# Attention over eight rows: 128x128 scores replaced by 32x32 diagonal blocks, with a block transpose on VectorE

## What is computed

```python
x -> layer_norm -> (S=8, B=512, D=256); H = 4 heads of 64
qkv = x @ Wqkv.T + bqkv
scores = einsum('bhqd,bhkd->bhqk', q, k) * (1/sqrt(64))   # 8 x 8 for each position and head
att = softmax(scores);  o = einsum('bhqk,bhkd->bhqd', att, v)
y = layer_norm(x + o @ Wo.T + bo);  idx = argmax(y @ Wg.T)   # the row's expert
```

## Time and profile before

| | us |
|---|---|
| median of 3 runs (lowest, highest) | 1231.37 (1230.73, 1235.14) |
| span of the profiled execution | 1231.3 |
| PE busy in the span | 1156.3 (94%) |
| DVE, ACT, POOL busy | 762.9 (62%), 529.5 (43%), 506.5 (41%) |
| mixing, 688.4 to 929 us | 240.6 |

### The profile page before, as it was taken

The page is one execution under the profiler, slowest core; times in us unless marked ns, Lnnn a source line. Parts: engine busy times, 40 slices in busy tenths (PEclk is TensorE's granted clock), DMA queues, the critical chain, the costliest instruction groups (busy, mean ns, idle before and its releaser), DMA issues. The chain is left out here.

```text
span 1231.3 us, 27541 instructions
## 1 busy us (share of the span) xinstructions
PE 1156.3 (94%) x8847; PEld 785.6 (64%) x8848; DVE 762.9 (62%) x2136; ACT 529.5 (43%) x1123; POOL 506.5 (41%) x718
## 2 busy tenths in 40 slices
PE   8999999999999999999898999999999999999995
PEld 3546455464554645546454466666667999999995
DVE  4555667757767577665635557666674565556653
ACT  5445454545454544545452255544433333333330
POOL 3334325244152442433421122444353556655664
PEclk9999999999999999999999999999999999999998
DMA  7284654644737346374273123434313111111110
GB/s 217 74 222 123 176 148 121 177 117 133 186 99 200 85 136 183 89 194 112 78 199 85 50 78 103 142 134 162 110 41 98 51 42 51 50 55 51 52 44 7
DMA packets 142637, 137.83 MB, mean 112 GB/s; under 512 B 29545, under 2 KB 135919, under 8 KB 142449
## 3 DMA queue, kind: packets, MB, share of 16 engines
q1 hardware_dynamic: 136976, 124.23, 36.2%
q0 software_dynamic: 5280, 12.66, 3.0%
q10 hardware_dynamic: 320, 0.16, 0.1%
HBM read 49.41 MB, written 50.83 MB: 81 GB/s over the span
## 5 line engine op out<-in xcount | busy, mean ns | idle before, releaser
L972 ACT ACTIVATE probs<-ps_b 128x512 f32<-128x512 f32 (+2 forms) x352 | 174.5, 538 | 91.8 <-PE ps_b L1439 36.5
L593 POOL TENSOR_SCALAR_AFFINE_SELECT probs<-probs 128x512 f32<-128x512 f32 x128 | 82.1, 641 | 267.8 <-ACT probs L972 264.5
L2840 PE MATMUL ps_c<-keep_w,e_hT 128*128 x624 | 141.0, 379 | 0.0
L2840 PEld LDWEIGHTS ps_c<-keep_w,e_hT 128*128 128x128 f32 x624 | 115.7, 190 | 14.1
L714 DVE CUSTOM_DVE_ANT_0 ps_a<-ps_a,mask_qk 128x256 f32<-128x256 f32 x224 | 88.9, 450 | 18.8 <-PE ps_a L1263 18.7
L708 DVE TENSOR_REDUCE top<-ps_a 128x2 f32<-128x512 f32 (+1 forms) x112 | 74.1, 683 | 30.1 <-PE ps_a L1263 29.3
L1263 PE MATMUL ps_a<-k_rows,q_rows 96*128 96x256 bf16 (+1 forms) x512 | 84.9, 262 | 4.6 <-DVE top L714 2.7
L1819 ACT ACTIVATE e_w_now<-keep_w 128x1024 f32 x78 | 78.1, 1049 | 22.0 <-issue 12.1
L2800 ACT ACTIVATE e_yT<-ps_d 128x256 f32<-128x256 f32 x39 | 14.9, 383 | 167.8 <-PE ps_d L2819 167.8
L2829 PE MATMUL ps_a<-e_yT,e_w_now 128*128 128x128 f32 x640 | 76.1, 278 | 0.0
L1294 PE MATMUL ps_b<-q_rows,k_rows 98*128 98x256 bf16 (+1 forms) x512 | 75.7, 261 | 0.2
(11 more groups left out here) (248 smaller groups left out, 2470.4 us busy)
## 6 DMA issues: line engine op xcount, KB each, us to landing
...
```

The lines of the kernel that those rows point to most:

```text
L593: nc.gpsimd.affine_select(own, own, [[0, TILES], [1, P]], ALU.is_ge, keep_zero, base=0, channel_multiplier=-1).then_inc(probs_cut.sem, 1)
L972: nc.scalar.activation(probs[:, user % 2, lo:lo + width], ps_exp[:, f % 2, 0:width], ACT.Exp).then_inc(exp_done.sem, 1)
L2840: mm = nc.tensor.matmul(ps_out[:, s, 0:D], hT[:, s, f, :], w2[:, bass.ds(e * KF * D + f * D, D)], start=(f == 0), stop=(f == KF - 1))
```

## The change

The rows of a tile are laid out by position (`x_in[s:P:B]`: row p is sequence row p % 8 of position p // 8), so the 8 rows of a position are neighbours and a 32x32 block on the diagonal holds four whole positions. Scores are computed for the four diagonal blocks of each tile and head alone: 64 matmuls of 32x32 for a group (`QUADS` = 4 blocks, `BLOCKS` = 16 tile-and-head pairs) with two mask products of 256 columns ahead of them, all into ps_c. So the whole group has 128x512 scores, where it had 128x2048. Softmax is done for the group at once in `shift_scores` (DVE: maximum, then subtract into SBUF), `exps` (one ACT Exp of 128x512), `normalise` (DVE: sum, reciprocal, multiply) and `turn`, now a DVE transpose within 32x32 blocks. `heads` is 64 matmuls of 32 rows by 64 columns by 32 into the joined tensor ps_ab, and ACT's `take_heads` moves them to oT in two operations.

PE's order changes with it: values of the next group are projected in the iteration before, features come directly behind scores, all four query and key products ahead of `heads`. DVE does `ln_statistics` between `shift_scores` and `normalise`, and `mix` behind `turn`. xnb gets two buffers, and mixed and yT buffers of their own; x is loaded one group further ahead. POOL and ACT build the mask once at the start of mixing. The token numbers are loaded in 8 strided transfers.

```diff
-PROJECT_FILLS = ["xT0", "xT1", "q0", "q1", "k0", "k1"]
-MIX_FILLS = ["out0", "out1", "v0", "v1", "xT0", "xT1", "q0", "q1", "yT0", "yT1", "logits", "k0", "k1", "ranks"]
+PROJECT_FILLS = ["xT0", "xT1", "q0", "q1", "k0", "k1", "v0", "v1"]
+MIX_FILLS = ["xT0", "xT1", "out0", "out1", "q0", "q1", "k0", "k1", "yT0", "yT1", "v0", "logits", "v1", "ranks"]
...
-        ps_pair, ps_turned, ps_work = (mem["ps_a"], mem["ps_b"]), mem["ps_c"], mem["ps_d"]
+        ps_heads, ps_scores, ps_work = mem["ps_ab"], mem["ps_c"], mem["ps_d"]
...
-                        sp.dma_start(x_in[s * POS:(s + 1) * POS, :, :],
+                        sp.dma_start(x_in[s:P:B, :, :],
                                      t["x2_groups"][m, s].rearrange("(c i) d -> i c d", i=POS)).then_inc(x_loaded.sem, 16)
...
-                    if work:
+                def iteration(n, ahead=True, more=True):
+                    if more:
+                        ln_first(n + 2)
+                    if ahead:
                         for h in range(2):
-                            pool.wait_ge(mixed_ready.sem, mixed_ready.count(n, h + 1))
-                            bias(n, h)
+                            if n > 0:
+                                pool.wait_ge(mixed_ready.sem, mixed_ready.count(n, h + 1))
+                            bias(n + 1, h)
...
+                def shift_scores(n):
+
+                    dve.wait_ge(scores_full.sem, scores_full.count(n, 1))
+                    ps = ps_scores[:, :, 0:BLOCKS // 2 * QUAD].rearrange("p o (b k) -> p o b k", k=QUAD)
+                    nc.vector.tensor_reduce(least[:, :, :], ps, AX.X, ALU.max, negate=True).then_inc(least_ready.sem, 1)
+                    dve.wait_ge(least_ready.sem, least_ready.count(n, 1))
+                    nc.vector.tensor_tensor(probs[:, :, :, :], ps, least[:, :, :].unsqueeze(3).broadcast_to(wide_blocks),
+                                            ALU.add).then_inc(shifted_ready.sem, 1)
+
+                def normalise(n):
+
+                    dve.wait_ge(exp_done.sem, exp_done.count(n, 1))
+                    nc.vector.tensor_reduce(total[:, :, :], probs[:, :, :, :], AX.X, ALU.add).then_inc(total_ready.sem, 1)
+                    dve.wait_ge(total_ready.sem, total_ready.count(n, 1))
+                    nc.vector.reciprocal(scale[:, :, :], total[:, :, :]).then_inc(scale_ready.sem, 1)
+                    dve.wait_ge(scale_ready.sem, scale_ready.count(n, 1))
+                    nc.vector.tensor_tensor(probs[:, :, :, :], probs[:, :, :, :],
+                                            scale[:, :, :].unsqueeze(3).broadcast_to(wide_blocks), ALU.mult
+                                            ).then_inc(probs_ready.sem, 1)
+
+                def turn(n):
+
+                    dve.wait_ge(probs_ready.sem, probs_ready.count(n, 1))
+                    if n > 0:
+                        dve.wait_ge(heads_full.sem, heads_full.count(n, 0))
+                    nc.vector.transpose(probsT[:, :, :, :].rearrange("p a b k -> p (a b k)"),
+                                        probs[:, :, :, :].rearrange("p a b k -> p (a b k)")).then_inc(turned.sem, 1)
...
-                    route = not (isinstance(n, int) and n == 0)
-                    maxima(n, 0)
-                    maxima(n, 1)
-                    normalise(n, 0)
+                def iteration(n, more=True):
+                    route = n > 0
+                    shift_scores(n)
+                    if more:
+                        ln_statistics(n + 2)
+                    normalise(n)
+                    turn(n)
                     if route:
                         mix(n, 0)
-                    normalise(n, 1)
-                    if route:
                         mix(n, 1)
-                    if route:
                         post_norm_statistics(n, whole)
-                    if project and route:
-                        dve.wait_ge(xnb_ready.sem, xnb_ready.count(n, 2))
-                        ln_apply(n + 1)
-                    if route:
                         post_norm_scale(n, whole)
-                    normalise(n, 2)
-                    if route:
                         post_norm_apply(n, 0, whole)
-                    normalise(n, 3)
-                    take_output(n, 0)
-                    take_output(n, 1)
                     if more:
-                        ln_statistics(n + 2)
+                        ln_apply(n + 2)
                     if route:
...
+                def exps(n):
+
+                    act.wait_ge(shifted_ready.sem, shifted_ready.count(n, 1))
+                    nc.scalar.activation(probs[:, :, :, :], probs[:, :, :, :], ACT.Exp).then_inc(exp_done.sem, 1)
...
+                def take_heads(n):
+
+                    act.wait_ge(heads_full.sem, heads_full.count(n, 1))
+                    for tile in range(KD):
+                        ps = ps_heads[:, :, TILES * QUAD * tile:TILES * QUAD * (tile + 1)]
+                        nc.scalar.activation(oT[:, tile, :].rearrange("p (c r q) -> p r c q", r=QUADS, q=QUAD),
+                                             ps.rearrange("p r (c q) -> p r c q", q=QUAD), ACT.Identity,
+                                             bias=b_v[:, tile:tile + 1]).then_inc(oT_ready.sem, 1)
 
                 def features(n):
...
-                    exps(n, 0)
-                    exps(n, 1)
-                    turn(n, 0)
-                    exps(n, 2)
-                    values(n, 0)
-                    values(n, 1)
-                    turn(n, 1)
                     if project:
                         features(n)
-                    exps(n, 3)
-                    turn(n, 2)
+                    exps(n)
                     if project:
                         queries(n)
+                        keys(n)
+                    take_heads(n)
                     if route:
...
+                    for c in range(TILES):
+                        for tile in range(KD):
+                            block = QUAD * (KD * c + tile)
+                            for odd in range(2):
+                                dims = slice(MD * odd, MD * (odd + 1))
+                                for r in range(QUADS):
+                                    own = slice(c * P + QUAD * r, c * P + QUAD * (r + 1))
+                                    mm = nc.tensor.matmul(ps_scores[QUAD * r:QUAD * (r + 1), odd, block:block + QUAD],
+                                                          qT[dims, tile, own], kT[dims, tile, own],
+                                                          start=False, stop=True, skip_group_check=True)
                     mm.then_inc(scores_full.sem, 1)
 
-                def probs_transposes(n, c):
-
-                    pe.wait_ge(probs_ready.sem, probs_ready.count(n, c + 1))
-                    pe.wait_ge(probsT_ready.sem, probsT_ready.count(n, c - 1))
-                    for h in range(MH):
-                        mm = nc.tensor.transpose(ps_turned[:, c % 2, h * P:(h + 1) * P], probs[:, c, h * P:(h + 1) * P], identf[:, :])
-                    mm.then_inc(turned.sem, 1)
...
+                def heads(n):
...
+                    for c in range(TILES):
+                        for tile in range(KD):
+                            for odd in range(2):
+                                h = 2 * tile + odd
+                                col = QUAD * (TILES * tile + c)
+                                for r in range(QUADS):
+                                    keys = slice(QUAD * r, QUAD * (r + 1))
+                                    mm = nc.tensor.matmul(ps_heads[MD * odd:MD * (odd + 1), r, col:col + QUAD],
+                                                          v[keys, c, MD * h:MD * (h + 1)], probsT[keys, odd, KD * c + tile, :],
...
 
-                    scores(n, 0)
-                    scores(n, 1)
+                    scores(n)
+                    if project:
+                        features(n)
                     if route:
                         output(n)
-                    if route:
-                        probs_transposes(n, 0)
-                    projected_values(n, 0)
-                    projected_values(n, 1)
-                    if not route:
-                        probs_transposes(n, 0)
-                    probs_transposes(n, 1)
                     if project:
-                        features(n)
-                    values(n, 0)
-                    if project:
-                        query_or_key(n, 0)
-                    probs_transposes(n, 2)
-                    values(n, 1)
-                    if project:
-                        query_or_key(n, 1)
+                        for j in range(4):
+                            query_or_key(n, j)
+                    heads(n)
                     if route:
                         y_features(n)
-                    probs_transposes(n, 3)
+                    if project:
+                        projected_values(n, 0)
                     if route:
```

(8 more changed lines are left out.)

247 lines of the change are left out of this document (108 added, 139 removed).

## The result

The changed kernel takes 1222.05 us (median of 4 runs, 1220.76 to 1223.48) against 1233.26 (1230.73 to 1235.83): ratio 0.990, interval 0.989 to 0.992. Forecast were 1205, measured -11 instead of -26. The sign and the range (1195 to 1228) held, the size did not: 60% of the expected gain is missing. The profiled execution spans 1220.8 us, 10.5 less than the one before.

The account below looks back on a forecast made before the run. PE's instruction count and block distances were taken to bound the mixing iteration. Six iterations -18.5, start -4.4, last iteration -4.3 and clock +1 gave -26.2 from 1231.3: 1205 us, range 1195 to 1228.

Parts of the forecast that it names:

- The tiny matmuls: Each group's 64 score and 64 value matmuls on PE: about 1.0 and 1.6 us, four places of the array working abreast.
- The path: Chain of waits through one full mixing iteration, PE and DVE steps: S + 6.5 + 6.9 + H + 7.5 = 24.05 us.
- the two new waits: PE waits 1.6 us for DVE's mix before the query products and 1.2 us for ACT's yT before projected values.
- the block transpose: DVE transpose of probabilities within 32x32 blocks: taken as an ordinary pass over 128x512, 0.69 us; no row showed one.
- Six iterations: 6 x (24.05 - 27.14) = -18.5: The six full mixing iterations each fall from 27.14 to 24.05 us, -18.5 us in all.
- the 1 us for the clock: PE idle over 4 us in the last iteration may drop the clock to 1.2 GHz, slowing the next products: 1 us added.
- SP's load of x for three groups ahead leaves behind DVE's ln_apply at about 15 and is wanted at 24.05 + 2.9 = 27: In each mixing iteration, x is loaded well before DVE wants it: no cost.
- my own sum for the start: Start of mixing through iteration 0: iteration 1 begins at 721.0 instead of 725.40, -4.4 us.
- The last iteration: Last mixing iteration, no projections, path on DVE: 15.9 us instead of 20.2, -4.3 us.
- the first: Rival: tiny matmuls cost 25 ns a record wherever they go, 28.7 us more, 1234, no change; 11%.
- the second: Rival: matmuls run one after the other, each waiting for its weight load, 10.2 us instead of 2.6, 1261; 8%.
- the third: Rival: DVE chain longer; a transpose as dear as the reciprocal gives 1226, a lock with POOL 1214; 14%.

Follow-up runs that it names:

- experiment 7: The changed kernel with the same 64 score and 64 value products ordered quarter by quarter of the array, not in turn: 1285.9 us, ratio 1.043.
- Experiment 4: The changed kernel with the coming group's statistics moved behind the present group's whole route on DVE, POOL's part likewise: 1212.5 us, ratio 0.984.
- Experiment 3: The changed kernel with POOL's four scatters of routed rows sent once the value products are done, not once yT is copied: 1218.0 us, ratio 0.990.
- experiment 9: The changed kernel with paced expert weights and earlier scatters, plus idle-filling products in PE's waits (16 in iteration 1, 5 and 16 in the last): 1214.2 us.
- Experiment 6: The changed kernel with statistics behind the route, paced expert weights and earlier scatters together: 1206.6 us, ratio 0.978.
- experiment 12: The changed kernel with idle-filling products (16 in iteration 1, 18 in the last), all expert weights held back until the last iteration's yT is copied: 1251.0 us.
- experiment 8: The changed kernel with later statistics, paced weights, earlier scatters, 18 idle-filling products, mix before turn and yT copied before the heads: 1206.1 us.

## Why the prediction was right on the iteration and wrong on the sum

**Right.** *The tiny matmuls*: 1.29 and 1.57 us for a forecast 1.0 and 1.6, by places working side by side, as the earlier trace rows had promised and the earlier trace rows had not; in experiment 7 the order alone makes them 2.7 and 4.2 times as long. *The path*: the two new waits are 1.37 (1.6) and 0.82 (1.2) us, the block transpose 0.71 (0.69), the multiply 0.69 in all iterations, where before it met POOL's bias once in each. The iteration is 23.96 (24.05).

**Wrong: "Six iterations: 6 x (24.05 - 27.14) = -18.5", and the 1 us for the clock.** I worked one iteration out and multiplied it. The measured six lose 13.7 against that:
- Iteration 1, +5.4. The step that failed is "SP's load of x for three groups ahead leaves behind DVE's ln_apply at about 15 and is wanted at 24.05 + 2.9 = 27", which I priced at nothing. For group 3 the load left on time, 14.1 us into iteration 0 (717.27). But iteration 0 has no route part and is only 16.1 us long (15.3 in my own sum for the start), so x was wanted at 19.4 and not at 27. It landed at 724.85, 2.26 us late, and that went straight into the DVE chain that I had put on the path: 2.3 us more wait, then 2.8 more for queries and keys at half the clock. Experiment 4 removed it.
- Iterations 3, 4: +2.5. The scatter's pause is no term of the sum at all. Experiment 3 removed it.
- Iteration 5, +6.7: the same pause; the stop for instructions, 2.08; and 4.4 for projected values and logits at half the clock, less 0.8, because the stop hid their wait for yT. The change doubles PE's records in mixing (1454 to 2885 matmuls), and with them the loads of 16 KB of instructions, 12 before and 23 after from 690 to 925 us (queue q8, below), and some fall where SP sends weights at 380 GB/s. I counted the tiny products' time and not that they have to be fetched.
- The last iteration, +4.3 (20.2 for 15.9): the scatter's pause 1.1 and the clock 2.0 (experiments 3 and 9). The remaining 1.2 is my own working: in experiment 9, at the full clock, y is complete 13.0 us into the iteration (12.4 in my sum), and what follows takes 4.2 (3.45), since the logits are done whole there and not by halves.
- Iterations 2 and 6 gave back 0.9. Iteration 6 has no coming statistics in the DVE chain, and its wait for mix is 0.43.
- The start gave back 1.9, and that was luck. Attention, whose program is the same, ran at half the clock twice for 3.41 us in the profile before (141.5 and 656.9 us; each put it 1.7 us behind) and never in the one after, so mixing's first transposes came 2.6 us sooner, as the lines below show. From them to iteration 1 it took 29.2 where my sum has 28.6.
- From output on, I had 1 us of loss for the clock, and 0.5 was measured: output took 6.31 us instead of 3.72, and the rest 2.1 less than before. Of these, 1.4 are luck too: before, the first expert's 32 products fell on a half-clock stretch (5.15 us for 3.74).

5.4 + 2.5 + 6.7 + 4.3 - 1.9 - 0.9 - 0.5 = 15.6, against the 15.7 that the profiled spans show (-10.5 for -26.2). Without the two pieces of luck the profiled gain would be some 4 us smaller: from the first transposes of xn to the output behind the last iteration, mixing went from 215.9 to 207.5 us, 8.4 less. The transposes before and after:

```profile
692.49 1.74 PE L2410 MATMUL ps_d<-m_identf,m_xn 128*128 128x128 f32 x8 [0.25 <-DVE m_xn L109]
```

```profile
689.89 1.97 PE L2408 MATMUL ps_d<-m_identf,m_xn 128*128 128x128 f32 x8 [0.45 <-DVE m_xn L109]
```

The text named the right alarms ("wrong if the first query product waits over 3 us, or if the granted clock falls inside the six iterations") and gave them no price: my cases had the clock in the last iteration alone. Of the rivals, the first (25 ns wherever they go) and the second are refuted by the rows above; the third had the right place, the DVE chain, and no lock: nothing in it was longer, x was late. My sum for iterations 1 to last is 6 x 24.05 + 15.9 = 160.2 for a measured 178.1. Experiment 6 reaches 158.3, but with a path 0.9 us shorter per iteration than the one forecast; no run has the forecast's order without its losses.

The loads of instructions, in the DMA views of 690 to 925 us (packets, MB, share), before and after:

```profile
q8 instruction: 12, 0.20, 0.3%
```

```profile
q8 instruction: 23, 0.38, 0.6%
```

What stays open: why, of 23 loads of instructions, only some stop PE. With the weights gone they stop it nowhere in the full iterations of experiment 12, but in experiments 6 and 8 one did so with all but idle DMA engines, inside a burst of 128 products. It is open too why the clock fell in busy stretches of experiment 7. How far ahead of use a load begins was not measured.
